# Last group's scores by key half, and the third group's divided values moved around them, in a conv-attention kernel

## What is computed

```
t = t + attn(ln(t)):  softmax(q k^T / sqrt(16) + bias(q - k)) v, then w_out, + b_out
t = t + ffn(ln(t)):   ln(t), + 2 in channels 32.. and 36.. at positions found by
                      comparing ln(t) > 0.5 in the fields at 0, 16, 20, 24, 39, 40
```

## Time and profile before

| what | value |
|---|---|
| device time, three runs | 53.51, 53.62, 53.62 us; median 53.62 us |
| the profiled execution | 53.42 us, its span 51.7 us |
| instructions | 1021 |
| mean granted TensorE clock | 0.967 of full speed |
| busy: PE / DVE / ACT / POOL | 40.9 / 40.2 / 28.6 / 23.5 us |
| chain that ended last: PE / DVE / POOL / ACT / issue / DMA | 35 / 24 / 13 / 10 / 7 / 6 % of the span |

### The profile page before, as it was taken

One profiled execution on the slowest core, in us unless ns is written; L12 is line 12 of the kernel. 1 busy time (PEld: TensorE's weight loads), 2 busy tenths in 40 slices (PEclk: granted clock), 3 DMA queues, 4 the chain that ended last, 5 costly groups with the idle time before them and its releaser, 6 DMA issues.

```text
span 51.7 us, 1021 instructions
## 1 busy us (share of the span) xinstructions
PE 40.9 (79%) x310; PEld 26.3 (51%) x312; DVE 40.2 (78%) x135; ACT 28.6 (55%) x63; POOL 23.5 (45%) x64
## 2 busy tenths in 40 slices
PE   0999899999996859649957996999994596996700
PEld 0332789685442645429824682599482352842500
DVE  2799778848983599999889999989999954699520
ACT  3600656395476768967998079339649900056020
POOL 4789432099999989736950031040029204016000
PEclk9999995569999999999999999999999999999999
DMA  0392400000000000000000000000000000002002
GB/s 0 80 304 42 35 5 0 0 0 0 0 0 6 0 0 0 0 6 13 6 0 0 0 0 0 0 13 0 0 0 0 0 0 0 0 0 101 1 0 101
DMA packets 1565, 0.92 MB, mean 18 GB/s; under 512 B 404, under 2 KB 1560, under 8 KB 1560
## 3 DMA queue, kind: packets, MB, share of 16 engines
q1 hardware_dynamic: 1104, 0.79, 4.9%
q10 hardware_dynamic: 456, 0.08, 1.7%
HBM read 0.60 MB, written 0.26 MB: 17 GB/s over the span
## 4 chain that ended last, share of the span: by engine, by line
PE 35%; DVE 24%; POOL 13%; ACT 10%; issue 7%; DMA 6%; POOLq 0%; DVEq 0%
PE ps L1013 8%; ACT probs L511 8%; DMA x_sb<-in_x_dram 6%; PE ps L994 5%; PE ps L963 4%; POOL stacks L303 4%; DVE negmax L761 4%; POOL stacks L304 4%; PE ps L996 4%; PE ps L935 3%; PE ps L1029 3%; PE ps L859 2%; POOL parts L310 2%; PE ps L913 2%; POOL wc L298 2%
## 5 line engine op out<-in xcount | busy, mean ns | idle before, releaser
L761 DVE TENSOR_REDUCE negmax<-ps 128x2 f32<-128x512 f32 x16 | 10.7, 675 | 0.8 <-PE ps L963 0.6
L511 ACT ACTIVATE probs<-ps 128x1024 f32<-128x1024 f32 x8 | 8.0, 1021 | 3.9 <-PE ps L996 3.9
L833 PE MATMUL ps<-warm 128*128 128x512 bf16 x28 | 8.9, 452 | 1.4 <-DVE warm L556 1.3
L994 PE MATMUL ps<-stacks 128*128 128x256 f16 x32 | 7.0, 273 | 0.0
L352 POOL TENSOR_TENSOR on<-pvq,rsum 128x256 f32<-128x256 f32 x3 | 1.8, 616 | 10.7 <-DVE rsum L683 10.7
L996 PE MATMUL ps<-qmk,ident 128*128 128x256 f16 (+1 forms) x32 | 6.6, 246 | 0.0
L963 PE MATMUL ps<-stacks 128*128 128x256 f16 x32 | 6.0, 274 | 0.2 <-ACT stacks L485 0.2
L833 PEld LDWEIGHTS ps<-warm 128*128 128x128 bf16 x30 | 3.2, 113 | 5.0 <-issue 2.2
L1013 PE MATMUL ps<-probs,v_aug 128*32 128x256 f32 x64 | 4.3, 384 | 1.7 <-ACT probs L511 1.5
L913 PE MATMUL ps<-wT,xtT 128*128 128x384 f32 x8 | 3.2, 505 | 0.7 <-ACT xtT L437 0.6
L994 PEld LDWEIGHTS ps<-stacks 128*128 128x128 f16 x32 | 3.1, 98 | 0.8 <-ACT stacks L492 0.4
(11 more groups left out here) (159 smaller groups left out, 94.4 us busy)
## 6 DMA issues: line engine op xcount, KB each, us to landing
x_sb<-in_x_dram SPq DMA_DIRECT2D x1, 256.0 KB, 2.9
out_dram<-y_sb SPq DMA_DIRECT2D x2, 128.0 KB, 1.7
wqkv_sb<-in_L_attn_w_qkv_dram SPq DMA_DIRECT2D x1, 192.0 KB, 3.0
wout_sb<-in_L_attn_w_out_dram SPq DMA_DIRECT2D x1, 64.0 KB, 3.3
bout_bc<-in_L_attn_b_out_dram ACTq DMA_DIRECT2D x1, 64.0 KB, 3.8
params<-in_L_conv_ln_w_dram ACTq DMA_DIRECT2D x1, 1.0 KB
params<-in_L_conv_ln_b_dram ACTq DMA_DIRECT2D x1, 1.0 KB
params<-in_L_conv_dt_w_dram ACTq DMA_DIRECT2D x1, 0.5 KB
```

Source lines behind the costliest of these rows:

```text
L511: act.activation(probs[:, 2 * c:2 * c + 2, :, :].rearrange("p h k q -> p (h k q)"), s2_ps[c % 2].rearrange("p a n -> p (a n)"), ACT.Exp, s ...
L761: dve.tensor_reduce(negmax[:, g, :, quadrant], s1_ps[h % 2].rearrange("p (q k) -> p q k", q=HALVES), AX_X, ALU.max, negate=True).then_inc( ...
L833: pe.matmul(ps[:, bank, :], warm[:, 0:P], warm[:], start=True, stop=True)
L994: pe.matmul(dst, kT[:, e, HW * b + P * t:HW * b + P * (t + 1)], qT[:, e, HW * b:HW * (b + 1)], start=True, stop=False)
```

## The change

The scores by key of the last group are no longer computed head by head in pairs, but key half by key half: first half 0 of all four heads into banks 2 and 3, then half 1 of all four into banks 4 and 5 (`last_scores_by_key`). ACT takes the exponentials of a half of all four heads in one instruction (`last_exponentials`). `values(3, 0)` waits for the first of them only. `values(2, 1)` moves behind these scores. ACT's `token_scale(0)` moves behind the exponentials. In DVE's list `find_channels(0)` moves ahead of `by_query(2)`, and `by_query(3)`, `invert(3)` ahead of `by_dim(2)`, `look_up(0)`. In POOL's list hot(0) moves ahead of on(2), and coefficients(0) behind on(3). Of the matmuls that keep PE busy before `project(1, [1])` three are left of five, and they now stand before `project(1, [0])`.

```diff
--- before.py
+++ after.py
@@ -32,7 +32,8 @@
 LN_EXP_SET = 6
 
 
-WARM_X, WARM_Z, WARM_SCAN, WARM_PV, WARM_OUT = 9, 1, 5, 5, 7
+WARM_X, WARM_Z, WARM_SCAN, WARM_PV, WARM_OUT = 9, 1, 5, 3, 7
+
 
 SHIFT_UNIT = 256.0
 SHIFT_PAIR = 1.4451980835487744e+17
@@ -173,6 +174,7 @@
         stacks_ps = [ps[:, bank, :].bitcast(F16).rearrange("p (o a t) -> p o a t", o=2, a=2) for bank in (6, 7, 6, 6)]
         s1_ps = [ps[:, 0, :], ps[:, 1, :]]
         s2_ps = [ps[:, 2:4, :], ps[:, 4:6, :]]
+        last_s2_ps = [ps[:, 2:4, :].rearrange("p k (a q) -> p (k a) q", q=HW), ps[:, 4:6, :].rearrange("p k (a q) -> p (k a) q", q=HW)]
         woutT_ps = ps[:, 7, 0:2 * P]
         mT_ps = ps[:, 7, 0:HW // 2].bitcast(F16)
         pv_ps = [ps[:, bank, 0:HW] for bank in (6, 6, 6, 7)]
@@ -347,28 +349,30 @@
                 for t in tiles(b):
                     pool.tensor_tensor(t1b[:, t, :], t1[:, t, :], bout_bc[:], ALU.add).then_inc(s_t1b, 1)
 
-            for g in range(NG - 1):
-                pool.wait_ge(s_rsum, g + 1)
-                pool.tensor_tensor(on[:, g, :, :], pvq[:, g, :, :],
-                                   rsum[:, g, :].unsqueeze(2).broadcast_to([P, HW // VW, VW]), ALU.mult)\
-                    .then_inc(s_on, 1)
-
-            for b in range(B):
+            def hot_fields(b):
                 ts = slice(HALVES * b, HALVES * (b + 1))
-                if b == 1:
-                    pool.wait_ge(s_rsum, NG)
-                    pool.tensor_tensor(on[:, NG - 1, :, :], pvq[:, NG - 1, :, :],
-                                       rsum[:, NG - 1, :].unsqueeze(2).broadcast_to([P, HW // VW, VW]), ALU.mult)\
-                        .then_inc(s_on, 1)
-                pool.wait_ge(s_frs, b + 1)
-                link(pool.tensor_scalar(neg_frs[:, ts], frs[:, ts], -1.0, 0.0, ALU.mult, ALU.add),
-                     pool.tensor_scalar(one_frs[:, ts], frs[:, ts], 1.0, 0.0, ALU.add, ALU.add))
-                pool.tensor_tensor(neg_fm[:, ts], fmv[:, ts, 0], neg_frs[:, ts], ALU.mult).then_inc(s_nfm, 1)
                 pool.wait_ge(s_above, b + 1)
                 link(pool.tensor_scalar(lift[:, ts], above[:, ts, SHL], 0.5, 0.5, ALU.mult, ALU.add))
                 pool.tensor_tensor(hot[:, ts, :, :], hot_at[:].unsqueeze(1).broadcast_to([P, HALVES, 2, D]),
                                    lift[:, ts].unsqueeze(2).unsqueeze(3).broadcast_to([P, HALVES, 2, D]), ALU.mult)\
                     .then_inc(s_hot, 1)
+
+            for g in range(NG):
+                if g == NG - 2:
+                    hot_fields(0)
+                pool.wait_ge(s_rsum, g + 1)
+                pool.tensor_tensor(on[:, g, :, :], pvq[:, g, :, :],
+                                   rsum[:, g, :].unsqueeze(2).broadcast_to([P, HW // VW, VW]), ALU.mult)\
+                    .then_inc(s_on, 1)
+
+            for b in range(B):
+                ts = slice(HALVES * b, HALVES * (b + 1))
+                pool.wait_ge(s_frs, b + 1)
+                link(pool.tensor_scalar(neg_frs[:, ts], frs[:, ts], -1.0, 0.0, ALU.mult, ALU.add),
+                     pool.tensor_scalar(one_frs[:, ts], frs[:, ts], 1.0, 0.0, ALU.add, ALU.add))
+                pool.tensor_tensor(neg_fm[:, ts], fmv[:, ts, 0], neg_frs[:, ts], ALU.mult).then_inc(s_nfm, 1)
+                if b == 1:
+                    hot_fields(b)
 
         @block.scalar
         def _(act):
@@ -504,6 +508,11 @@
                 for t in tiles(b):
                     act.activation(t3[:, t, :], t2[:, t, :], ACT.Identity, bias=neg_fm[:, t:t + 1],
                                    scale=one_frs[:, t:t + 1]).then_inc(s_t3, 1)
+
+            def last_exponentials(t):
+                act.wait_ge(s_s2, 2 * NG - 1 + t)
+                act.activation(probs[:, HG * (NG - 1):HG * NG, t, :], last_s2_ps[t],
+                               ACT.Exp, scale=DECAY).then_inc(s_exp, 1)
 
             def exponentials(c):
 
@@ -528,12 +537,14 @@
             exponentials(0)
             even_stacks(3)
             exponentials(1)
-            for g in range(1, NG):
+            for g in range(1, NG - 1):
                 even_shifts(g)
-                if g == NG - 1:
-                    token_scale(0)
                 exponentials(2 * g)
                 exponentials(2 * g + 1)
+            even_shifts(NG - 1)
+            last_exponentials(0)
+            last_exponentials(1)
+            token_scale(0)
             plus_normalised(0)
             token_scale(1)
 
@@ -805,14 +816,14 @@
             residual(0)
             odd_shifts(3)
             token_stats(0)
+            dve.wait_ge(s_consts, 9)
+            find_channels(0)
             by_query(2)
             invert(2)
-            dve.wait_ge(s_consts, 9)
-            find_channels(0)
+            by_query(3)
+            invert(3)
             by_dim(2)
             look_up(0)
-            by_query(3)
-            invert(3)
             by_dim(3)
             one_hots(0)
             residual(1)
@@ -997,6 +1008,20 @@
                 if h % 2 == 1:
                     last.then_inc(s_s2, 1)
 
+            def last_scores_by_key():
+                b = B - 1
+                pe.wait_ge(s_mre, NG)
+                pe.wait_ge(s_mro, NG)
+                for t in range(HALVES):
+                    pe.wait_ge(s_exp, 2 * NG - 3 + t)
+                    for a in range(HG):
+                        e = HEADS - HG + a
+                        dst = last_s2_ps[t][:, a, :]
+                        pe.matmul(dst, kT[:, e, HW * b + P * t:HW * b + P * (t + 1)], qT[:, e, HW * b:HW * (b + 1)],
+                                  start=True, stop=False)
+                        last = pe.matmul(dst[:, P * t:HW], ident16[:], qmk[:, 0:HW - P * t], start=False, stop=True)
+                    last.then_inc(s_s2, 1)
+
             def values(g, t):
 
                 b = g // 2
@@ -1008,7 +1033,7 @@
                 else:
                     pe.wait_ge(s_odd, NG - 1)
                     pe.wait_ge(s_even, NG - 1)
-                pe.wait_ge(s_exp, 2 * g + 2)
+                pe.wait_ge(s_exp, 2 * g + 2 if g < NG - 1 else 2 * g + 1 + t)
                 for j in range(HG):
                     last = pe.matmul(pv_ps[g][VW * j:VW * (j + 1), :],
                                      v_aug[:, 2 * b + t, HG * (g % 2) + j, :], probs[:, HG * g + j, t, :],
@@ -1099,13 +1124,12 @@
             project(0)
             shift_rows(3)
             values(2, 0)
+            last_scores_by_key()
             values(2, 1)
-            for h in range(HG * (NG - 1), HG * NG):
-                scores_by_key(h)
             values(3, 0)
             values(3, 1)
+            keep_warm(WARM_PV, 2)
             project(1, [0])
-            keep_warm(WARM_PV, 2)
             project(1, [1])
             output(0)
             keep_warm(WARM_OUT, 2)
```

More of the change, by code:

```diff
@@ L348, in _ @@
                     pool.tensor_tensor(t1b[:, t, :], t1[:, t, :], bout_bc[:], ALU.add).then_inc(s_t1b, 1)
-            for g in range(NG - 1):
+            def hot_fields(b):
+                ts = slice(HALVES * b, HALVES * (b + 1))
+                pool.wait_ge(s_above, b + 1)
+                link(pool.tensor_scalar(lift[:, ts], above[:, ts, SHL], 0.5, 0.5, ALU.mult, ALU.add))
+                pool.tensor_tensor(hot[:, ts, :, :], hot_at[:].unsqueeze(1).broadcast_to([P, HALVES, 2, D]),
+                                   lift[:, ts].unsqueeze(2).unsqueeze(3).broadcast_to([P, HALVES, 2, D]), ALU.mult)\
+                    .then_inc(s_hot, 1)
+            for g in range(NG):
+                if g == NG - 2:
+                    hot_fields(0)
                 pool.wait_ge(s_rsum, g + 1)
```

## The result

The changed kernel took 53.25 us (median of 20 executions; 53.56 us for the kernel before, measured beside it): ratio 0.9957, 95% interval 0.9942 to 0.9973. It is faster, by 0.43% or 0.23 us. The forecast was 0.14 us, and 53.48 us.

The account below looks back on a forecast made before the run. One chain of dependent steps bounds the kernel, decided by when by_dim(3) starts. 0.23 - 0.12 + 0.53 - 0.50 = 0.14 us gained, so 53.48 us from 53.62; range 53.15 to 53.88.

Parts of the forecast that it names:

- Scores earlier: Last group's scores on PE, with values(2, 1) behind them: first matmul at 37.38 against 37.61, 0.23 us gained.
- The wider half 0: Half 0 of four heads' scores on PE takes longer than a pair of heads: 0.12 us lost.
- Exponentials: ACT's last two exponentials have as many elements as before and take the same 1.95 us.
- Half of the values off the path: Only values(3, 1) remains on PE behind the second exponential: 0.53 us gained.
- The gap behind invert(3): by_dim(2) and look_up(0) now precede by_dim(3) on DVE: 0.50 us lost, 0.30 by queue length, 0.20 by POOL.
- DVE free for by_query(3): DVE finishes invert(2) at 40.35, before by_query(3) at 41.23, with 0.9 us to spare.
- Small POOL operations: Three coefficient operations beside look_up(0): cost between 0 and 0.25 us, taken as 0; rival of about 0.15 more, chance 0.12.
- Coefficients behind on(3): POOL makes coefficients(0) from 42.62, and ACT t3 from 43.5, in time for output(0): hidden.
- side by side: Rival: DVE and POOL run concurrently behind invert(3), by_dim(3) at 42.95, 53.28 us; chance 0.22.
- The transpose as part of the exclusion: Rival: by_dim(2) on DVE shuts out POOL's on(3), by_dim(3) at 43.55, 53.88 us; chance 0.07.
- The clock: Rival: PE idles more with two fillers less and drops to 1.2 GHz, about 54.0 us; chance 0.06.

Follow-up runs that it names:

- halves_reversed: lookup_early with the last group's two key halves in the other order, half 1 first; ratio to the kernel before 0.9801.
- order_alone: The changed kernel with the last group's scores, exponentials and values head by head as before, values(3, ...) waiting for both exponentials; ratio to the kernel before 1.0017.
- lookup_early: The changed kernel with look_up(0) moved in DVE's list from behind by_dim(2) to before by_query(2); ratio to the kernel before 0.9857.
- lookup_gap: The changed kernel with look_up(0) moved in DVE's list to directly before by_query(3); ratio to the kernel before 0.9938.
- pool_reads: lookup_early with one added POOL product of two SBUF tiles behind hot(0), its result unread; ratio to the kernel before 0.9897.
- pool_writes: lookup_early with one added POOL memset, which only writes, behind hot(0); ratio to the kernel before 0.9863.
- no_fill: The changed kernel without its three filler matmuls before project(1, [0]); ratio to the kernel before 0.9922, from two executions.
- half_alone: The kernel before with only the last group's scores and exponentials by key half, values(3, 0) waiting for the first exponential; ratios 0.9969 and, run again, 0.9942.

## Why the prediction was right

The direction, the place and the mechanism were as forecast; the size was 0.14 us, the traces have 0.20, the first measurement 0.23 (interval 0.14 to 0.31). Step by step:

- *Scores earlier*, 0.23: from the end of even_shifts(3) to the first score PE took 0.06 us in the changed kernel, before 37.61 - 37.24 = 0.37. So 0.31. The 0.13 us between ACT's end and PE's start, read off the exponentials, did not hold for this copy; this term was mis-sized by 0.08, and the trace of before had rows of both kinds (last section).
- *The wider half 0*, -0.12: from the first score to the exponentials 40.03 - 38.95 = 1.08 against 0.98. So -0.10. halves_reversed shows the same from the other side: 0.22 us earlier with half 1 first.
- *Exponentials*: 1.95 as before. Right.
- *Half of the values off the path*, 0.53: from the start of the exponentials to `by_query(3)` 2.78 instead of 3.28 us. So 0.50. Only 0.43 of it is the half itself: order_alone, with all 16 records behind the exponentials, has 4.24 - 1.03 = 3.21. The other 0.07 is the shorter step from PE to `by_query(3)`, which the prediction did not have.
- *The gap behind invert(3)*, -0.50: 1.93 instead of 1.42 us from `by_query(3)` to `by_dim(3)`. So -0.51, and lookup_early gives it back (5.85 to 5.33). That POOL holds up the look-up rested on four rows in the prediction; lookup_gap, pool_reads and pool_writes show it. But the split of the term, 0.30 by the length of DVE's list and 0.20 by POOL, was wrong, and that the two add up so well is luck. The first look-up instruction took 0.48 us, where 0.3 was expected, since it started earlier beside on(3). `by_dim(2)` started at 43.42, 0.61 behind `by_query(3)` and not 0.72, and ended at 43.82. From there look_up(0) would have taken 41.41 - 40.90 = 0.51 us as before, to 44.33, and `by_dim(3)` would have started near 44.36, which is 1.55 behind `by_query(3)`. By this estimate from the rows about 0.13 is the list's own length and 0.38 is POOL's.
- *DVE free for by_query(3)*: 0.76 us idle before it; the forecast had 0.9. *Small POOL operations*: L754 took 0.19 instead of 0.16, so 0.03 at most. *Coefficients behind on(3)*: ready at 44.83, 0.63 us behind its end, and no one on the path waited for them.

Sum of what was measured: 0.31 - 0.10 + 0.50 - 0.51 = 0.20 us.

Of the rivals, side by side falls by the stretched look-up and by lookup_gap. The transpose as part of the exclusion falls too: `by_dim(2)` ran from 43.42 to 43.82 while on(3) started at 43.58, neither stretched. The clock did not fall on this stretch in the changed kernel's profile, but it did in that of no_fill, where PE had idled for 1.20 us and then again for up to 0.69. So the prediction's reason against it, that the clock had held through 1.35 us of an idle PE, was no safe bound.

What the prediction did not ask is whether the reordering of the lists was needed. It treats it as part of the change and prices it; half_alone shows that the key halves alone come out 0.12 us ahead of the whole change by the trace. Nor did it ask for another place for look_up(0), which was worth more than the whole change.

## What to carry to other kernels

When a wait on the critical path is shortened, look at what the other engines have queued in the gap it left: work that once filled idle time for nothing becomes the path, and moving four small instructions to an earlier gap was worth more (0.5 us) than the whole change. Before a DVE instruction with two SBUF inputs is put beside a POOL instruction, see whether that one reads SBUF; even an operation on two elements waits for its end. When work is split to let half of it start early, put the cheaper half first (0.21 us here, by the trace).

## What was not expected of the hardware

- From the end of ACT's copy of 64 x 512 elements (even_shifts(3)) to PE's first dependent matmul there were 0.06 us, from the end of ACT's exponential of 128 x 1024 to PE 0.14, in the same execution. The chain of the kernel before has both values behind copies of ACT, so the kind of ACT's operation does not decide it; what does is open:

```profile
17.16 0.59 ACT stacks L485
17.74 0.05 issue
17.79 0.61 PE ps L963 x4
...
18.66 0.38 ACT xtT L437
19.04 0.14 issue
19.17 0.88 PE ps L913 x2
```

- A granted clock that fell to 0.50 at 43.6 us in no_fill's trace was still there from 45.00 to 47.00, although PE was busy for 2.00 of these 2.00 us. In the ten microseconds before the fall PE had not been idle for more than 1.20 us at a stretch. The lower clock cost 1.8 us at the end, most of it in fillers that stand in front of needed work.
- A DVE operation on two elements of each partition took 0.57 us beside a POOL product that reads SBUF (lookup_gap), and 0.16 us in lookup_early with POOL idle.
